# Graph attention on one core: the exponentials of a step issued before that step's node matrices, and the break in the turn of three banks moved from units 15 and 1 to units 11 and 13

## The chip, the cores and the metric

The kernel runs on one core of one Trainium2 chip. A core has a matrix engine (TensorE, in the profile PE, its weight loads PEld), VectorE (DVE), ScalarE (ACT), GpSimd (POOL) and a queue engine (SyncE, SP). Each runs its own list of instructions in order and waits for the others through semaphores. The metric is the time of one execution on the device in microseconds (us). Of the kernel before there are three runs, and one more execution that the profiler watched.

## The reference

The input is a graph of 6250 nodes with 256 features and 106250 edges, sorted by their receiving node. First comes a layer norm, then graph attention with four heads of 64 features, two batch norms with a feed-forward layer between them, and a layer of eight experts. The change lies in the attention:

```python
xl = (x @ W_l).reshape(n, H, C)
xr = (x @ W_r).reshape(n, H, C)
feat = xl[src] + xr[dst]
feat = jnp.where(feat >= 0, feat, NEG_SLOPE * feat)
logits = jnp.einsum('ehc,hc->eh', feat, att)
seg_max = jax.ops.segment_max(logits, dst, num_segments=n)
ex = jnp.exp(logits - seg_max[dst])
seg_sum = jax.ops.segment_sum(ex, dst, num_segments=n)
alpha = ex / (seg_sum[dst] + 1e-16)
out = jax.ops.segment_sum(alpha[:, :, None] * xl[src], dst, num_segments=n)
```

## The kernel before

Edges are packed in tiles of 128, and two tiles that end in the same block of 128 nodes are a unit. Sixteen units are a chunk, and there are 29 chunks. The attention (`attend`) is a software pipeline over steps: step c computes the logits of chunk c, the softmax of chunk c-1, and the weighted sums of chunks c-2 and c-1. Each engine runs its own list of it. A step has sixteen places h = 0 to 15.

- GpSimd gathers the rows `xl[src]` of the two tiles of a unit with two indirect DMAs (L822), five units ahead of the logits. Before that it waits until the sums of the unit that held the same place in the ring are done (`sum_done`).
- SyncE loads the block's rows `xr` (L849).
- ScalarE builds one-hot matrices. For a group of four tiles (a quad, two units) `near_nodes` (L880) and `hot_nodes` (L886) give the node matrix `hot_n`, and `near_edges` (L896) and `hot_edges` (L903) give the edge matrix `hot_e`. `hot_nodes` of quad j waits for `f_done` of the units of quad j-2, since `hot_n` has two buffers. Once a step `exponents` (L921) takes the exponential of the logits less their peak, and `fade_factor` (L925) that by which older sums are scaled down. A step of ScalarE has eight places j, one for two units.
- TensorE at place h makes `logits_of` (L1139 and L1141) for unit h into a PSUM bank of `f_ps`, then `sums_of` (L1154) for an older unit hh = (h + 7) mod 16 into a bank of `o_ps`. At h = 1 it turns the logits (`turn_logits`, L1163) and at h = 6, between logits and sums, the weights (`turn_weights`, L1172 to L1175). The latter waits for the exponentials and the factor.
- VectorE at place h does `settle` (L997, from a bank of `f_ps`), `add_up` (L1034, from a bank of `o_ps`), `messages` (L1021) and `logits_of` (L1007, a reduction). The softmax follows it in three parts at h = 1, 2, 3. The last part ends with L1083, the input of `fade_factor`. At h = 6 VectorE also takes the turned weights (L1014).

`f_ps` and `o_ps` have three banks each. Sixteen is not a multiple of three, so the turn 0, 1, 2 has to break once in a chunk. `slot(h)` says which bank unit h uses, and `freed_by(h)` which earlier unit must have been read by VectorE before TensorE may write that bank. Everywhere but at the break that is the unit three before. With the turn of the kernel before, unit 15 takes bank 1 and waits for unit 13, and unit 1 of the next chunk waits for unit 15: two before in both. Units 0 and 2 wait for the unit four before. The same two functions serve the logits (unit h, at place h) and the sums (unit hh, at place hh - 7 mod 16). `wait_past(pe, settled, ...)` (L1136) and `wait_past(pe, added, ...)` (L1152) are the waits.

Of the kernel before, what the change touches and what calls it, by code (L numbers as in the profile page):

```python
# [37 lines left out]
NU = T // 2  # L38
# [644 lines left out]
def attend(nc, k):  # L683
# [19 lines left out]
    assert NCH % 2 == 1 and NU % LANDS == 0 and T == 32 and NU == 16  # L703


    slot = lambda h: 1 if h == NU - 1 else h % 3
    freed_by = lambda h: h - (4, 2, 4)[h] if h < 3 else h - 2 if h == NU - 1 else h - 3
    with ExitStack() as ctx:
        sb = lambda name, shape, dt=F32: ctx.enter_context(nc.sbuf_tensor(name, shape, dt))
        pb = lambda name, shape: ctx.enter_context(nc.psum_tensor(name, shape, F32))  # L710
# [78 lines left out]
        def has_logits(c):  # L789

            return not isinstance(c, int) or c < NCH

        def softmax_in(c):

            return not isinstance(c, int) or 1 <= c <= NCH

        def behind(c, h, lag):

            b = max(0, -((h - lag) // NU))
            if isinstance(c, int) and not 0 <= c - b < NCH:  # L800
                return None
            return c - b, b, h - lag + b * NU

        def ring_half(engine, c):

            return nc.values_load_multi_w_load_instructions(k.parity[:, bass.ds(c, 2)], engines=[engine], min_val=0, max_val=1)[1]

        with nc.Block(no_gpsimd_drain=True) as block:
# [50 lines left out]
            def _(act):  # L859
# [3 lines left out]
                def relative_rows(c, j):  # L863

                    wait_past(act, far_n_ready, c * QUADS + (j - 2))
                    at = (c * T + j * QT) * P
                    act.dma_start(rel_bc[:, j // 2 % 2].rearrange("p q t e -> p (q t e)"),
                                  k.rel_rows[bass.ds(at, 2 * QT * P)].partition_broadcast(P)).then_inc(rel_in[j // 2 % 2], 16)
# [6 lines left out]
                def near_nodes(c, j):  # L875

                    if j % 2 == 0:
                        act.wait_ge(rel_in[j // 2 % 2], c * (4 * QUADS) + (j // 4 + 1) * 16)
                    wait_past(act, hot_n_ready, c * QUADS + j)
                    nc.scalar.activation(far_n[:, :, :], rel_bc[:, j // 2 % 2, j % 2], ACT.Abs, bias=k.neg_col[:, 0:1]).then_inc(far_n_ready, 1)  # L880

                def hot_nodes(c, j):

                    act.wait_ge(far_n_ready, c * QUADS + (j + 1))
                    wait_past(act, f_done, c * NU + 2 * (j - 1))
                    nc.scalar.activation(hot_n[:, j % 2], far_n[:, :, :], ACT.Relu, scale=-1.0,  # L886
                                         bias=k.one[:, 0:1]).then_inc(hot_n_ready, 1)
# [18 lines left out]
                def linear_parts(c, half):  # L906
                    act.wait_ge(f_done, c * NU)
                    wait_past(act, rows_done, c - 1)
                    act.sem_inc(k.taken, 1)
                    nc.scalar.copy(linear[:, :, :], half.rearrange("p t (h w) -> p h t w", w=XC)[:, :, :, C]).then_inc(linear_ready, 1)  # L910

                def side_masks(c):
                    for i in range(2):
                        nc.scalar.activation(side[:, i], rel_r[:, bass.ds(c - 1, 1), :].rearrange("p o e -> p (o e)"),
                                             ACT.Abs, scale=-1.0, bias=ends[:, i, bass.ds(c - 1, 1)]).then_inc(sides_ready, 1)
                    act.wait_ge(sides_ready, 3 * c - 1)
                    nc.scalar.activation(side[:, :, :], side[:, :, :], ACT.Copy, scale=-NEG).then_inc(sides_ready, 1)

                def exponents(c):
                    act.wait_ge(soft, (c - 1) * SOFT + 12)  # L920
                    nc.scalar.activation(expo[:, 0], below_peak[:, :], ACT.Exp).then_inc(expo_ready, 1)  # L921

                def fade_factor(c):
                    act.wait_ge(soft, (c - 1) * SOFT + 14)
                    nc.scalar.activation(faded[:, :], off_lane[:, :], ACT.Exp, bias=fade[:, 0:1]).then_inc(faded_ready, 1)  # L925

                def step(c):
                    soft_in = softmax_in(c)
                    if isinstance(c, int):
                        other, ring = (c + 1) % 2, xl_e[:, (c + 1) % 2 * T:(c + 1) % 2 * T + T, :]  # L930
                    else:
                        other = ring_half(mybir.EngineType.Activation, c)[1]
                        ring = xl_e.rearrange("p (s t) w -> p s t w", s=2)[:, bass.ds(other, 1)].rearrange("p o t w -> p (o t) w")
                        other = bass.ds(other, 1)
                    for j in range(QUADS):
                        last = j + 1 == QUADS
                        quad = (c + last, (j + 1) % QUADS) if has_logits(c + last) else None
                        edges = behind(c, 2 * j + 3, SUM)
                        if edges:
                            edges = edges[0], edges[2] // 2  # L940
                        if quad:
                            near_nodes(*quad)
                            hot_nodes(*quad)
                            if quad[1] % 2:
                                ahead = (quad[0] + (quad[1] + 3) // QUADS, (quad[1] + 3) % QUADS)
                                if has_logits(ahead[0]):
                                    relative_rows(*ahead)
                        if soft_in and j == 0:
                            linear_parts(c, ring)
                            side_masks(c)  # L950
                        if soft_in and j == 3:
                            exponents(c)
                            fade_factor(c)
                        if edges:
                            near_edges(*edges)
                        if edges:
                            hot_edges(*edges)
                        if has_logits(c) and j == 3:
                            gates_of(c)
                        if j == 4 and has_logits(c + 1):  # L960
                            if not isinstance(c, int) or c > 0:
                                act.wait_ge(f_done, c * NU)
                            target = idx[:, other, :]
                            nc.scalar.copy(target if isinstance(c, int) else target.rearrange("p o t -> p (o t)"),
                                           k.src_e[:, bass.ds((c + 1) * T, T)]).then_inc(idx_ready, 1)
# [4 lines left out]
                near_nodes(0, 0)  # L970
                hot_nodes(0, 0)
                steps_alone(act, step)

            @block.vector
# [1298 lines left out]
```

## Time and profile before

| | |
|---|---|
| three runs | 2504.38, 2498.19, 2502.48 us, median 2502.48 us |
| the profiled execution | 2508.43 us, its span 2506.6 us, granted clock 0.886 |
| busy in the span: PE, DVE, ACT, POOL | 79%, 60%, 48%, 48% |
| indirect gathers L822 | 928, 960 ns each |
| logits' matmuls L1139, L1141 | 1856 and 1856, 391 and 402 ns |
| settle L997, messages L1021, reduction L1007 | 464 each, 681, 679, 681 ns |

Matmuls overlap, so a PE that is busy may still be idle in parts. "idle before" in a row is the time in which that engine did nothing before the instruction, and the name behind it is what ended it by the profile. "issue" and "remote" stand where the profile names no engine.

### The profile page before, as it was taken

The numbers are of one execution on the slowest core, as the hardware profiler recorded it, in microseconds if no ns is written. First come the engines' busy times: TensorE is split into PE (matmuls) and PEld (weight loads), VectorE is DVE, ScalarE is ACT, GpSimd is POOL, SyncE is SP. The second block draws the span as 40 slices with busy tenths as digits, with TensorE's granted clock in tenths as the row PEclk, the third lists the DMA queues.
The fourth block names the chain that finished last, engine by engine and source line by source line (L and its number), as shares of the span: only waits on it lengthen the run. The fifth ranks groups of instructions, "written<-read, shape, count | busy, mean of one in ns | idle before, by whom it ended". The sixth has DMA issues, their size and how long they took to land. (4 is left out here: it accounts for less than half of the span.)

```text
span 2506.6 us, 43475 instructions
## 1 busy us (share of the span) xinstructions
PE 1984.4 (79%) x9692; PEld 1690.5 (67%) x9693; DVE 1516.3 (60%) x3638; ACT 1191.0 (48%) x2805; POOL 1214.0 (48%) x1207
## 2 busy tenths in 40 slices
PE   2974788878888888878888888887886626999996
PEld 2763666767777676767676776667875525888885
DVE  5964777777777777777778777788456440111110
ACT  2542555555555555555555555655545412232321
POOL 3346656555666556655656565520002551344444
PEclk9988998998989899998989899988985557999998
DMA  7675666666666666666666666626602335666664
GB/s 210 228 250 180 193 186 195 185 188 183 194 187 188 180 189 191 194 182 188 189 184 195 176 191 187 190 68 188 204 7 90 108 120 166 136 145 141 144 143 76
DMA packets 256713, 422.34 MB, mean 168 GB/s; under 512 B 45802, under 2 KB 128089, under 8 KB 256653
## 3 DMA queue, kind: packets, MB, share of 16 engines
q1 hardware_dynamic: 154608, 223.36, 28.4%
q0 software_dynamic: 65408, 153.31, 24.9%
q10 hardware_dynamic: 36636, 45.00, 5.6%
q8 instruction: 23, 0.38, 0.1%
q14 instruction: 38, 0.30, 0.0%
HBM read 358.65 MB, written 62.86 MB: 168 GB/s over the span
## 5 line engine op out<-in xcount | busy, mean ns | idle before, releaser
L822 POOL DMA_INDIRECT ring<-xl_rows,a_idx x928 | 890.5, 960 | 594.1 <-issue 272.4
L1139 PE MATMUL a_f_ps<-a_xr_w,a_hot_n 128*128 128x256 f32 x1856 | 571.4, 391 | 177.1 <-DVE a_pos L997 77.8
L1141 PE MATMUL a_f_ps<-ring,ident 128*128 128x256 f32 x1856 | 591.3, 402 | 0.4 <-issue 0.4
L1139 PEld LDWEIGHTS a_f_ps<-a_xr_w,a_hot_n 128*128 128x128 f32 x1856 | 368.0, 203 | 280.5 <-issue 165.1
L1154 PE MATMUL a_o_ps<-ring,a_hot_e 128*128 128x264 f32 x1856 | 535.3, 415 | 19.4 <-issue 13.4
L1154 PEld LDWEIGHTS a_o_ps<-ring,a_hot_e 128*128 128x128 f32 x1856 | 377.0, 207 | 94.0 <-issue 26.5
L997 DVE SCALAR_TENSOR_TENSOR a_pos<-a_f_ps,att_cols 128x512 f32<-128x512 f32 x464 | 316.2, 681 | 190.8 <-remote 120.9
L903 ACT ACTIVATE a_hot_e<-a_far_e,one 128x512 f32<-128x512 f32 x232 | 167.6, 723 | 444.0 <-PE a_o_ps L1154 247.2
L1007 DVE TENSOR_REDUCE a_lg<-a_pos 128x8 f32<-128x512 f32 x464 | 316.0, 681 | 25.2 <-remote 14.9
L1021 DVE TENSOR_TENSOR ring<-ring,a_sm_ps (+1 forms) x464 | 315.2, 679 | 1.7 <-issue 1.7
L1141 PEld LDWEIGHTS a_f_ps<-ring,ident 128*128 128x128 f32 x1856 | 305.6, 202 | 1.2 <-issue 1.1
L896 ACT ACTIVATE a_far_e<-iota_row,a_near_rel 128x128 f32<-128x128 f32 x928 | 294.9, 389 | 4.6 <-issue 3.4
L1034 DVE TENSOR_TENSOR acc<-a_o_ps,acc 128x264 f32 x464 | 198.0, 427 | 159.9 <-PE a_o_ps L1154 80.4
L2033 POOL DMA_INDIRECT out_dram<-ring,x_idx x106 | 166.0, 1566 | 262.8 <-issue 125.1
L886 ACT ACTIVATE a_hot_n<-a_far_n,one 128x512 fp32r<-128x512 f32 x232 | 167.7, 723 | 199.0 <-remote 90.6
L2152 DVE CAST x_idx<-ring 128x2 int32<-128x2 f32 x53 | 9.1, 171 | 386.8 <-PE x_y_ps L2079 386.8
L2079 PE MATMUL x_y_ps<-we,ring 128*128 x848 | 191.6, 379 | 0.0
L2069 PE MATMUL x_hid_ps<-ring,x_w 128*128 128x256 f32 x784 | 177.2, 379 | 0.0
L880 ACT ACTIVATE a_far_n<-a_rel_bc,neg_col 128x512 f32<-128x512 bf16 x232 | 164.9, 711 | 23.1 <-issue 19.5
L2079 PEld LDWEIGHTS x_y_ps<-we,ring 128*128 128x128 f32 x848 | 157.1, 190 | 19.3
L2069 PEld LDWEIGHTS x_hid_ps<-ring,x_w 128*128 128x128 f32 x784 | 149.0, 190 | 20.3
L2111 ACT COPY ring<-x_zt_ps 128x512 f32<-128x512 f32 x53 | 31.1, 586 | 249.7 <-PE x_zt_ps L2047 170.0
(349 smaller groups left out, 2206.3 us busy)
## 6 DMA issues: line engine op xcount, KB each, us to landing
a_xr_w<-xr_rows SPq DMA_DIRECT2D x464, 256.0 KB
a_rel_bc<-rel_rows ACTq DMA_DIRECT2D x116, 256.0 KB
x_w<-in_L_ffn_W_dram SPq DMA_DIRECT2D x57, 512.0 KB, 4.2
ring<-xl_rows,a_idx POOLq DMA_INDIRECT x928
xr_rows<-xr_parts SPq DMA_DIRECT2D x50, 256.0 KB, 2.1
ring<-disp_rows SPq DMA_DIRECT2D x49, 257.0 KB
xl_rows<-xl_sb SPq DMA_DIRECT2D x50, 132.0 KB, 1.8
j_xl<-xl_rows SPq DMA_DIRECT2D x25, 264.0 KB, 2.9
```

The lines of the kernel that those rows point to most:

```text
L822: nc.gpsimd.indirect_dma_start(xl_e[:, p * T + 2 * h + u, :], None, k.xl_rows, bass.IndirectOffsetOnAxis(ap=idx[:, p, 2 * h + u:2 * h + u ...
L886: nc.scalar.activation(hot_n[:, j % 2], far_n[:, :, :], ACT.Relu, scale=-1.0, bias=k.one[:, 0:1]).then_inc(hot_n_ready, 1)
L896: nc.scalar.activation(far_e[:, u, :], k.iota_row[:, :], ACT.Abs, bias=near_rel[:, j * QT + u:j * QT + u + 1]).then_inc(far_e_ready, 1)
L997: nc.vector.scalar_tensor_tensor(pos[:, h % 2], f_ps[:, slot(h)], 0.0, att, ALU.max, ALU.mult).then_inc(settled, 1)
L1007: nc.vector.tensor_reduce(lg[:, :, 2 * h:2 * h + 2].rearrange("p h t -> p t h"), pos[:, h % 2].rearrange("p t (h c) -> p t h c", c=C), AX. ...
L1021: nc.vector.tensor_tensor(at[:, :, :, 0:C], at[:, :, :, 0:C], exs_of(sm)[:, 2 * hh:2 * hh + 2, :, None].to_broadcast([P, 2, H, C]), ALU.mu ...
L1034: nc.vector.tensor_tensor(at, o_ps[:, slot(hh), 0:XW], at, ALU.add).then_inc(added, 1)
L1139: nc.tensor.matmul(f_ps[:, slot(h), u, :], hot_n[:, j % 2, 2 * g + u, :], xr_w[:, h % XR, a, :].bitcast(F32R), start=(a == 0), stop=False)
L1141: last = nc.tensor.matmul(in_heads(f_ps[:, slot(h), u, :]), k.ident[:, :], heads_of(xl_e[:, p * T + 2 * h + u, :])[:, :, 0:C], start=False ...
L1154: last = nc.tensor.matmul(o_ps[:, slot(hh), 0:XW], hot_e[:, j % 2, 2 * g + u, :], xl_e[:, pp * T + 2 * hh + u, :], start=(u == 0), stop=(u ...
L2069: last = nc.tensor.matmul(hid_ps[:, q % 2, j], w1[:, q % RING, h, j * P:(j + 1) * P], zt[:, q % 2, h], start=(h == 0), stop=(h == DH - 1))
L2079: last = nc.tensor.matmul(y_ps[:, q % 2, u], hid[:, q % 2, j, u * P:(u + 1) * P], k.we2[:, bass.ds(e[u], 1), j, :].rearrange("p o n -> p ( ...
```

## The change

Two edits, both in the attention.

The first moves the calls of `exponents(c)` and `fade_factor(c)` in ScalarE's place j = 3. They stood behind `near_nodes` and `hot_nodes` of quad 4, and now stand ahead of them. The second gives `slot` and `freed_by` a start of the turn behind unit 11. Unit 12 has bank 0, 13 bank 1, and so on over the chunk's end, up to unit 10 with bank 2; unit 11 has bank 1. So unit 11 now waits for unit 9 and unit 13 for unit 11 (two before), units 12 and 14 for the unit four before, and all others, 15 and 1 too, for the unit three before. It holds for logits and sums alike.

```diff
-    slot = lambda h: 1 if h == NU - 1 else h % 3
-    freed_by = lambda h: h - (4, 2, 4)[h] if h < 3 else h - 2 if h == NU - 1 else h - 3
+    CLOSE = 11
+    turn_of_slots = lambda h: (h - CLOSE - 1) % NU
+    slot = lambda h: 1 if h == CLOSE else turn_of_slots(h) % 3
+    freed_by = lambda h: h - (4, 2, 4)[turn_of_slots(h)] if turn_of_slots(h) < 3 else h - 2 if h == CLOSE else h - 3
...
                         quad = (c + last, (j + 1) % QUADS) if has_logits(c + last) else None
+                        if soft_in and j == 3:
+                            exponents(c)
+                            fade_factor(c)
                         edges = behind(c, 2 * j + 3, SUM)
...
                             side_masks(c)
-                        if soft_in and j == 3:
-                            exponents(c)
-                            fade_factor(c)
                         if edges:
                             near_edges(*edges)
```

On ScalarE, in the repeated step, this is what stands between the edge matrix of place j = 2 and the edge matrices of place j = 3 in the kernel before:

```order
L903 ACTIVATE a_hot_e<-a_far_e,one 128x512 [waits a_sum_s]
L878 REGISTER_ALU
L880 ACTIVATE a_far_n<-a_rel_bc,neg_col 128x512 [waits a_hot_n_s,a_rel_in0]
L884 REGISTER_ALU
L125 REGISTER_ALU [waits a_far_n_s]
L886 ACTIVATE a_hot_n<-a_far_n,one 128x512 [waits a_f_s]
L920 ISA
L921 ACTIVATE a_expo<-a_below_peak 128x128 [waits a_soft]
L924 REGISTER_ALU
L925 ACTIVATE a_faded<-a_off_lane,a_fade 128x5 [waits a_soft]
L125 REGISTER_ALU
```

And in the changed kernel (its lines are two further down):

```order
L905 ACTIVATE a_hot_e<-a_far_e,one 128x512 [waits a_sum_s]
L922 ISA
L923 ACTIVATE a_expo<-a_below_peak 128x128 [waits a_soft]
L926 REGISTER_ALU
L927 ACTIVATE a_faded<-a_off_lane,a_fade 128x5 [waits a_soft]
L880 REGISTER_ALU
L882 ACTIVATE a_far_n<-a_rel_bc,neg_col 128x512 [waits a_hot_n_s,a_rel_in0]
L886 REGISTER_ALU
L125 REGISTER_ALU [waits a_far_n_s]
L888 ACTIVATE a_hot_n<-a_far_n,one 128x512 [waits a_f_s]
L125 REGISTER_ALU
```

The two exponentials, which wait for VectorE's softmax (`a_soft`), have moved past the node matrix, which waits for TensorE's logits (`a_f_s`). No DMA moved past another.

On TensorE, at place h = 6 of the repeated step, the kernel before has this between the logits of unit 6 and those of unit 7:

```order
L1139 MATMUL a_f_ps<-a_xr_w,a_hot_n 128x256 x2
L1141 MATMUL a_f_ps<-ring,ident 128x256
L1171 ISA [waits a_expo_s,a_faded_s,a_soft,a_masks]
L1172 MATMUL a_sm_ps<-a_faded,a_spot 128x5 [waits a_spot_s]
L1173 MATMUL a_sm_ps<-a_lane,a_spot 128x5
L1175 MATMUL a_sm_ps<-ident,a_expo 128x128 x2
L1154 MATMUL a_o_ps<-ring,a_hot_e 128x264 [waits a_added,a_msg_s]
L1154 MATMUL a_o_ps<-ring,a_hot_e 128x264
```

The changed kernel has there:

```order
L1141 MATMUL a_f_ps<-a_xr_w,a_hot_n 128x256 x2
L1143 MATMUL a_f_ps<-ring,ident 128x256
L1170 REGISTER_ALU [waits a_masks]
L1173 ISA [waits a_faded_s,a_expo_s,a_soft]
L1174 MATMUL a_sm_ps<-a_faded,a_spot 128x5 [waits a_spot_s]
L1175 MATMUL a_sm_ps<-a_lane,a_spot 128x5
L1177 MATMUL a_sm_ps<-ident,a_expo 128x128 x2
L1156 MATMUL a_o_ps<-ring,a_hot_e 128x264 [waits a_added,a_msg_s]
L1156 MATMUL a_o_ps<-ring,a_hot_e 128x264
```

No matmul moved. What the second edit changes is the bank that a matmul writes and the count that it waits for, which these rows don't tell.

## Rows read from the trace of the kernel before

**Rows 1.** Busy time in windows: steps 2 to 27, then step 24 alone.
```profile
core 0: us, PE busy (x) PEld busy (x) DVE busy (x) ACT busy (x) POOL busy (x), PEclk, DMA share, GB/s
282.10:1613.00 1330.90, 1090.90 (x5254) 921.04 (x5253) 1019.50 (x2158) 736.65 (x1664) 796.26 (x831) 0.91 0.64 188
1413.10:1460.00 46.90, 39.88 (x205) 33.63 (x203) 37.52 (x82) 27.88 (x64) 28.81 (x31) 0.96 0.67 201
```
**Rows 2.** Who waited for whom over the whole span: us in total, times, longest.
```profile
POOL ring L822 <- PE a_o_ps L1154: 227.6, 115, 2.8
PEld a_sm_ps L1172 <- issue: 120.4, 29, 5.7
ACT a_hot_n L886 <- remote: 90.6, 18, 10.1
PE a_f_ps L1139 <- DVE a_pos L997: 77.8, 27, 10.0
```
**Rows 3.** Timeline of step 20, places 5 to 7: start, us, instruction, idle before.
```profile
1225.67 0.15 DVE L1083 TENSOR_TENSOR a_fade<-a_reach_t,a_peak 128x1 f32<-128x1 f32 x1
...
1228.44 0.72 ACT L886 ACTIVATE a_hot_n<-a_far_n,one 128x512 fp32r<-128x512 f32 x1 [7.33 <-remote]
...
1229.27 0.28 ACT L925 ACTIVATE a_faded<-a_off_lane,a_fade 128x5 f32<-128x5 f32 x1
...
1229.78 0.59 PE L1172 MATMUL a_sm_ps<-a_faded,a_spot 128*128 128x5 f32 x2 [5.07 <-ACT a_faded L925]
...
1232.51 1.00 PE L1139 MATMUL a_f_ps<-a_xr_w,a_hot_n 128*128 128x256 f32 x2
...
1233.40 0.43 DVE L1034 TENSOR_TENSOR acc<-a_o_ps,acc 128x264 f32 x1 [2.14 <-PE a_o_ps L1154]
```
**Rows 4.** Timeline of step 3, the same place.
```profile
355.25 0.15 DVE L1083 TENSOR_TENSOR a_fade<-a_reach_t,a_peak 128x1 f32<-128x1 f32 x1
...
355.98 0.38 PE L1172 MATMUL a_sm_ps<-a_faded,a_spot 128*128 128x5 f32 x2 [1.70 <-DVE a_expo L1082]
...
357.39 0.70 PE L1139 MATMUL a_f_ps<-a_xr_w,a_hot_n 128*128 128x256 f32 x2
```
**Rows 5.** The same pair in the first and last of the steps 2 to 27.
```profile
302.91 0.15 DVE L1083 TENSOR_TENSOR a_fade<-a_reach_t,a_peak 128x1 f32<-128x1 f32 x1
...
306.91 0.59 PE L1172 MATMUL a_sm_ps<-a_faded,a_spot 128*128 128x5 f32 x2 [4.96 <-ACT a_faded L925]
...
1584.28 0.15 DVE L1083 TENSOR_TENSOR a_fade<-a_reach_t,a_peak 128x1 f32<-128x1 f32 x1
...
1587.69 0.58 PE L1172 MATMUL a_sm_ps<-a_faded,a_spot 128*128 128x5 f32 x2 [4.36 <-ACT a_faded L925]
```
**Rows 6.** Timeline of step 20: settle 13 and logits 15, then step 21, logits 1.
```profile
1251.99 0.68 DVE L997 SCALAR_TENSOR_TENSOR a_pos<-a_f_ps,att_cols 128x512 f32<-128x512 f32 x1
...
1252.73 0.51 PE L1139 MATMUL a_f_ps<-a_xr_w,a_hot_n 128*128 128x256 f32 x2 [0.92 <-issue]
...
1260.46 0.68 DVE L997 SCALAR_TENSOR_TENSOR a_pos<-a_f_ps,att_cols 128x512 f32<-128x512 f32 x1
...
1261.29 0.47 PE L1139 MATMUL a_f_ps<-a_xr_w,a_hot_n 128*128 128x256 f32 x2 [2.24 <-issue]
...
1261.99 0.69 DVE L1007 TENSOR_REDUCE a_lg<-a_pos 128x8 f32<-128x512 f32 x1
...
1263.12 0.64 PE L1163 MATMUL a_sm_ps<-ident,a_lg 128*128 128x128 f32 x2
```
**Rows 7.** Step 20: logits 13 and settle 11 (places 13 and 11).
```profile
1247.01 0.59 PE L1139 MATMUL a_f_ps<-a_xr_w,a_hot_n 128*128 128x256 f32 x2
...
1247.74 0.68 DVE L997 SCALAR_TENSOR_TENSOR a_pos<-a_f_ps,att_cols 128x512 f32<-128x512 f32 x1
```
**Rows 8.** Step 20: sums 11 and add 9 (places 4 and 2).
```profile
1218.31 1.05 PE L1154 MATMUL a_o_ps<-ring,a_hot_e 128*128 128x264 f32 x4
...
1219.80 0.42 DVE L1034 TENSOR_TENSOR acc<-a_o_ps,acc 128x264 f32 x1
```

## The prediction, made before the changed kernel ran

> **What bounds the kernel now.** I read the busy times in windows first. The attention's steps 2 to 27 take 1330.9 us together, which is 51.2 us for each of 26 steps and half of the span; nothing outside the attention is changed. TensorE is busy 1090.9 us of them, VectorE 1019.5, GpSimd 796.3, ScalarE 736.7 [rows 1]. None is busy all the time: the engines take turns waiting for each other. One step of the 26 took only 46.9 us with the same work [rows 1], so the waits can be smaller without any work being removed. The list of waits says where they are [rows 2]. TensorE's sequencer stood 120.4 us before the turn of the weights (L1172), once in each of 29 steps, 4.15 us each time. TensorE stood 77.8 us more before the logits' matmuls for VectorE's settle, and ScalarE 90.6 us before `hot_nodes`, on a signal that the profile gives no engine for. The reader is to see that the turn of the weights is the largest single stop of TensorE, and that it depends on an instruction that ScalarE has queued behind `hot_nodes`.
>
> The timeline of step 20 shows why [rows 3]. VectorE ends the softmax's last part at 1225.82 (1225.67 + 0.15). ScalarE is free, but its next instruction is `hot_nodes`, which starts at 1228.44 after 7.33 us of standing; only then come the exponential and the factor (ends 1229.55), and the turn starts at 1229.78, 3.96 us after the softmax's end. VectorE then loses 2.14 us before its `add_up` at place 6, whose matmuls are queued behind the turn. In step 3 the same way from the softmax's end (355.40) to the turn (355.98) took 0.58 us [rows 4]. That is the shortest that I find, and what an exponential without another wait ahead of it costs.
>
> **Edit 1, the exponentials first.** Over the 26 steps the way from softmax's end to the turn is 2.03 us in the mean: 3.85 in the first, 3.26 in the last [rows 5], 0.57 to 0.60 in 8 of them and more in 18. With `exponents` ahead of `near_nodes` and `hot_nodes` the only thing ahead that waits for TensorE is the edge matrix of place 2, and with that step 20's ScalarE was done by 1221.11 (1228.44 - 7.33). So the way falls to about 0.58 everywhere: 2.03 - 0.58 = 1.45 us a step, 42 us for 29 steps. Bounds: nothing, if what VectorE and TensorE do next starts no earlier; and 120.4 us, all of the stop before the turn, which it can't reach because most of the stop is the softmax itself. What the edit delays is the node matrix of quad 4. It takes two instructions of about 0.72 us, so it would end some 1.8 us after the softmax's end. Its first reader is the logits of unit 8, and before these come the turn, sums 13, logits 7 and sums 14; in step 20 the turn alone to logits 7 is 1229.78 to 1232.51, 2.7 us [rows 3]. That covers it, and I cost it at nothing. If the cover were gone, each step would lose at most the 1.4 us of the two instructions.
>
> How much of the 1.45 us arrives at the end? TensorE stands ahead of the turn, so it starts sums 13 earlier by all of it. VectorE waits there for sums 13 in the steps of the late kind (2.14 us in step 20, rows 3) and not in the others. Against this I set the lengths of whole steps: the 8 steps with the short way took 49.8 us in the mean, the 18 others 52.2. The difference of 2.4 us is even a little more than the 2.1 us by which their ways differ (2.68 - 0.58), though other things differ in these steps too. So I take the full 42 us.
>
> **Edit 2, the break of the turn.** Four places of TensorE wait for a bank at the break: logits 15 and 1 and sums 15 and 1 before, logits 11 and 13 and sums 11 and 13 now.
> - Logits 15 (waits for settle 13). In step 20 settle 13 ends at 1252.67 and logits 15 starts at 1252.73 after 0.92 us of idling [rows 6]. In all 26 steps it starts 0.05 us after that settle, and the idling is 1.92 us in the mean. This wait goes; the next is settle 12.
> - Logits 1 (waits for settle 15). In step 21 settle 15 ends at 1261.14, logits 1 starts at 1261.29 after 2.24 us. So it is in 18 of 26 steps, mean idle 1.70 us. This wait goes too, but the turn of the logits (L1163) is behind it in the queue and needs the reduction of unit 15, which ends at 1262.68; the turn starts at 1263.12 [rows 6]. At most 0.44 us is to be had here in that step, 0.24 in most.
> - Logits 13 (now waits for settle 11). In step 20 it starts at 1247.01 and settle 11 ends at 1248.42 [rows 7]. In all 26 steps logits 13 started before that settle's end, by 1.41 us in the mean. So TensorE will stand about 1.4 us there, more if edit 1 makes it earlier. From logits 13 to the point where TensorE is ready for logits 15 it is 4.80 us (1252.73 - 0.92 - 1247.01) in step 20, and settle 13 ends 4.25 us after settle 11. So in such a step logits 15 would start about 0.5 us later than now, not earlier. Where VectorE has stood between settle 11 and settle 13 (9 of 26 steps have an idle of 2.8 us or more ahead of logits 15) TensorE no longer stands with it, and I put that at 2 us. The mean is (9 x 2 - 17 x 0.5) / 26 = 0.37 us gained, rounded to 0.3.
> - Logits 11 (now settle 9) has 0.99 us to spare in the mean and would wait in 6 of 26 steps. Sums 13 (now add 11) has 1.98 us to spare.
> - Sums 11 (now waits for add 9). In step 20 it starts at 1218.31 and add 9 ends at 1220.22 [rows 8]; it started early in 23 of 26 steps, by 1.30 us in the mean. The delay passes to logits 5, sums 12 and logits 6. All of that is in front of the turn of the weights, where TensorE stands 4.15 us now and would still stand 4.15 - 1.45 = 2.7 us with edit 1. So it is hidden.
>
> Bounds for the whole edit: the two waits that go are worth at most 1.92 + 0.24 = 2.2 us a step; the two that come cost at most 1.41 + 1.30 = 2.7. I take the 0.3 us a step from logits 15, 9 us, close to nothing, because the wait at 13 gives back most of what the wait at 15 took.
>
> **The sum.** 42 + 9 = 51 us off the profiled execution's 2508.4 (its span is 2506.6, so 1.8 us lie around it): 2457. The median of the three runs is 6 us lower, so the same saving gives 2502.5 - 51 = 2451. Since both terms lean to their favourable side I name 2455.
>
> **Rivals.**
> - *The clock comes back* (larger gain). After 5.07 us of standing the first matmul pair of logits 7 takes 1.00 us where a pair takes 0.5 elsewhere [rows 3, 6], and from the turn to logits 7 it is 2.73 us against 1.41 us in step 3, where TensorE stood 1.70 us [rows 3, 4]. Those are the levels of 1.2 and 2.4 GHz; the granted clock is 0.91 over the steps and 0.96 in the quickest one [rows 1]. With the stop split between sums 11 and a shorter wait at the turn, 1.3 us more a step come back, 38 us: 2413. Against it: VectorE has to use the earlier sums. The Trainium skill, TensorE: Matmul & The Clock Gate, "What's actually happening", says "the default state is throttled, and activity releases the throttle". By that rule shorter stops give clock back, which is this rival; the rows just named agree.
> - *Hidden anyway* (no change). GpSimd stood 227.6 us for sums that TensorE had to signal [rows 2], and in step 20 ScalarE got the signal of logits 5 only at 1228.4, although TensorE had been through with logits 6 since 1224.71 (1229.78 - 5.07, rows 3). If these late signals set the pace of everything, the turn comes earlier and VectorE waits for the next signal instead: 2500. For it: 7.33 us of waiting in rows 3 are not explained by work. Against: the short-way steps are shorter.
> - *The wait at 13 and 11 costs* (slower). Place: logits 13 and sums 11. TensorE's lead over VectorE is cut to two units there, and if late signals reach VectorE meanwhile it runs dry. Price: 1.41 + 1.30 - 0.3 - 0.24 = 2.2 us a step, 63 us. It decides when edit 1 brings less than that, because sums 11 isn't hidden: with the 42 us in full the sum is +21 us, 2523. It needs sums 11 to delay settle 4 or the softmax; in step 20 VectorE reached the softmax's end without waiting for TensorE, which speaks against it.
> - *The exponential is late for another reason* (the edit doesn't do what it says): the edge matrix ahead of it waits for TensorE as well, and if its signal is as late as that of `hot_nodes`, half of the 42 us are lost: 2475. This lies within the forecast's own range.
>
> **How the numbers follow.** Forecast (with the last rival) 0.46, own range 2430 to 2485; clock 0.15, 2395 to 2430; hidden 0.19, 2485 to 2510; slower 0.20, 2510 to 2545. The likeliest gives 2455. From 2412 to 2520 leaves out about 1 in 10 on each side. No change can be told from one within 0.3%, that is 2495 to 2510. Faster: 0.46 + 0.15 + 0.06 of the hidden case = 0.67; same 0.12; slower 0.21.
>
> **What would show it.** Right: the way from L1083's end to the turn is near 0.6 us in all steps; the sequencer's stop before the turn falls from 120 to about 75 us; logits 15 and 1 start without idling and logits 13 starts 0.05 us after settle 11; the steps average 49.4 us. Wrong in edit 1: the turn is early but VectorE's idle time per step is unchanged, or ScalarE's exponential waits behind the edge matrix. Wrong in edit 2: sums 11's wait lengthens the way to the softmax, or VectorE idles more at places 13 to 15 than before.

## The result and the profile after

The changed kernel takes 2484.74 us (median of 4 runs, 2481.26 to 2486.9) beside 2503.43 us for the kernel before (4 runs, 2498.19 to 2504.71): a ratio of 0.9932, 95% interval 0.9912 to 0.9952. It is faster by 18.7 us, 0.7%. The forecast was 2455 us, 48 us less than before. The profiled execution took 2486.9 us, its span is 2485.1 us, the granted clock 0.904.

The same kernel before took 2479 to 2503 us in some groups of runs (called late below; the result above and the profile ahead of the prediction are of this kind) and 2156 to 2158 us in others (called quick), whatever version ran beside it, so every ratio below is within one group.

Busy time in the changed kernel's windows, the 26 steps and then step 20, in the columns of [rows 1]:

```profile
280.69:1596.63 1315.94, 1057.66 (x5254) 891.77 (x5253) 1016.62 (x2161) 740.55 (x1665) 796.45 (x833) 0.95 0.64 190
1194.71:1243.96 49.25, 39.01 (x205) 33.62 (x203) 37.57 (x82) 27.67 (x63) 29.42 (x32) 0.97 0.64 188
```

A step is 50.61 us in place of 51.19: the 26 steps give 15.0 of the 21.5 us between the spans, the steps and drains around them 4.4, the rest of the program 2.2. The granted clock rose from 0.91 to 0.95 and TensorE is busy 33 us less, but VectorE's idle time fell only from 11.98 to 11.51 us a step.

The list of waits of the changed kernel answers to [rows 2]:

```profile
POOL ring L824 <- PE a_o_ps L1156: 195.7, 112, 2.9
...
PE a_f_ps L1141 <- DVE a_pos L999: 97.4, 38, 10.7
...
PEld a_sm_ps L1174 <- issue: 49.5, 24, 4.8
```

TensorE's sequencer stands 49.5 us before the turn of the weights where it stood 120.4. TensorE's wait for the settle rose from 77.8 to 97.4. The waits moved from the turn to the logits.

The timeline of step 20 around the softmax answers to [rows 3]:

```profile
1215.21 0.31 ACT L923 ACTIVATE a_expo<-a_below_peak 128x128 f32<-128x128 f32 x1 [2.07 <-issue]
1215.30 0.15 DVE L1085 TENSOR_TENSOR a_fade<-a_reach_t,a_peak 128x1 f32<-128x1 f32 x1
...
1216.02 0.38 PE L1174 MATMUL a_sm_ps<-a_faded,a_spot 128*128 128x5 f32 x2 [1.31 <-ACT a_expo L923]
```

In this step ScalarE waits for the softmax and not for TensorE. The turn starts 0.57 us after the softmax's end (1215.45), where it took 3.96 us before, and the node matrix follows at once (1216.50). The edit does what it says. But seven microseconds later in the same step:

```profile
1222.98 0.59 PE L1143 MATMUL a_f_ps<-ring,ident 128*128 128x256 f32 x2
...
1225.20 0.59 PE L1143 MATMUL a_f_ps<-ring,ident 128*128 128x256 f32 x2
...
1228.04 0.96 POOL L824 DMA_INDIRECT ring<-xl_rows,a_idx  x1 [0.30 <-issue]
1230.84 0.69 DVE L999 SCALAR_TENSOR_TENSOR a_pos<-a_f_ps,att_cols 128x512 f32<-128x512 f32 x1 [3.24 <-remote]
1230.84 0.72 ACT L888 ACTIVATE a_hot_n<-a_far_n,one 128x512 fp32r<-128x512 f32 x1 [3.62 <-remote]
1231.58 0.80 PE L1141 MATMUL a_f_ps<-a_xr_w,a_hot_n 128*128 128x256 f32 x2 [4.89 <-DVE a_pos L999]
1231.75 0.95 POOL L824 DMA_INDIRECT ring<-xl_rows,a_idx  x1 [2.75 <-remote]
```

TensorE ended logits 9 at 1223.57 and logits 10 at 1225.79. VectorE's settle of unit 9 waits for that signal until 1230.84, 7.3 us after the work, and ScalarE's node matrix is let go at the same moment. Logits 11, which after edit 2 waits for settle 9, stands 4.89 us behind it. The trace has the two signals at 1230.81 and 1230.96. They came while GpSimd had stopped (1229.00 to 1231.75), after an unbroken row of eight gathers.

Counted over the 416 units of steps 2 to 27, by the records of TensorE's signals for logits (some records of late ones are missing): 115 of 416 are on time, that is within 0.3 us of the matmul's modelled end. Of those due in the first 1.3 us of a row of gathers 29 of 42 are, of those due 3.9 us or more into a row none of 168. Of 215 late arrivals on record 196 fall in a stop of GpSimd, 1.7 us (median) after its last gather ended. All 50 settles ahead of which VectorE idled over 1.5 us started in such a stop or less than 1 us behind it; they are 5.7 us a step. In the kernel before it was 122 of 416 on time and 38 such settles, 4.6 us a step.

The Trainium skill, Perfetto Trace Analysis, "Tensor Engine Instruction (MATMUL, LD_WEIGHTS)", says that the matmul's end in a trace is an estimate and that the signal goes out later. That alone doesn't explain 7.3 us here: TensorE's next logits followed 2.2 us after logits 9, at the usual pace, and where signals are on time they are within 0.3 us of that estimated end.

### The profile page after: what moved, and what is told of

Read it like the earlier page. It is cut to its first block and busy times, and to the rows that moved or that the text cites. A ratio compares the mean times of both kernels' runs of the same rounds, so it can differ in the third digit from the quotient of the medians.

```text
span 2485.1 us, 43501 instructions
## 1 busy us (share of the span) xinstructions
PE 1949.5 (78%) x9692; PEld 1661.9 (67%) x9693; DVE 1512.5 (61%) x3638; ACT 1193.7 (48%) x2805; POOL 1211.4 (49%) x1207
## 2 busy tenths in 40 slices
DMA packets 256712, 422.34 MB, mean 170 GB/s; under 512 B 45801, under 2 KB 128088, under 8 KB 256652
## 5 line engine op out<-in xcount | busy, mean ns | idle before, releaser
L1141 PE MATMUL a_f_ps<-a_xr_w,a_hot_n 128*128 128x256 f32 x1856 | 572.5, 391 | 156.4 <-DVE a_pos L999 97.4
L1156 PE MATMUL a_o_ps<-ring,a_hot_e 128*128 128x264 f32 x1856 | 521.9, 406 | 60.1 <-DVE acc L1036 35.9
L1156 PEld LDWEIGHTS a_o_ps<-ring,a_hot_e 128*128 128x128 f32 x1856 | 364.1, 201 | 140.1 <-issue 79.7
```

The costliest lines, as they stand in the source:

```text
L1141: nc.tensor.matmul(f_ps[:, slot(h), u, :], hot_n[:, j % 2, 2 * g + u, :], xr_w[:, h % XR, a, :].bitcast(F32R), start=(a == 0), stop=False)
L1156: last = nc.tensor.matmul(o_ps[:, slot(hh), 0:XW], hot_e[:, j % 2, 2 * g + u, :], xl_e[:, pp * T + 2 * hh + u, :], start=(u == 0), stop=(u ...
```

## GpSimd's row of gathers and its stops

The gathers' own group, in the kernel before and then in the changed one. Behind the bar stand busy us and mean ns of one, behind the next bar the idle time ahead of them and what ended it.

```profile
L822 POOL DMA_INDIRECT ring<-xl_rows,a_idx x928 | 890.5, 960 | 594.1 <-issue 272.4 <-PE a_o_ps L1154 227.6 <-remote 80.4
```
```profile
L824 POOL DMA_INDIRECT ring<-xl_rows,a_idx x928 | 888.1, 957 | 578.8 <-issue 248.5 <-PE a_o_ps L1156 195.7 <-remote 121.8
```

Busy and idle together fell from 1484.6 to 1466.9 us, 17.7 of the 21.5 us between the spans. A gather shows 0.96 us and then 0.30 of "issue" even within a row, so 32 gathers take GpSimd 40.4 us a step (1.262 us each). In the 26 steps it counts as busy for 60% (796.3 of 1330.9 us), but the gathers with these gaps are 79% of a step. With its stops (idle over 0.6 us, each counted beyond the 0.30) this gives the step:

| kernel, late groups | stops a step | their time | 40.4 + stops | step measured |
|---|---|---|---|---|
| before | 6.6 | 10.70 | 51.1 | 51.19 |
| changed | 5.7 | 10.21 | 50.6 | 50.61 |
| changed, second group | 5.4 | 10.04 | 50.4 | 50.49 |
| exponentials alone | 5.3 | 10.12 | 50.5 | 50.43 |
| break alone | 5.8 | 9.81 | 50.2 | 50.17 |
| lead limited | 5.5 | 10.48 | 50.9 | 50.76 |

This is bookkeeping and not a cause: the gathers and the idle time between them fill a step whatever sets its length, so the sum would come out in any version. The experiments without gathers test the cause.

## The experiments

### The edits taken apart, quick group

All cuts of code are against the changed kernel unless said otherwise. The exponentials alone (edit 1, the turn of banks as before):

```diff
-    CLOSE = 11
-    turn_of_slots = lambda h: (h - CLOSE - 1) % NU
-    slot = lambda h: 1 if h == CLOSE else turn_of_slots(h) % 3
-    freed_by = lambda h: h - (4, 2, 4)[turn_of_slots(h)] if turn_of_slots(h) < 3 else h - 2 if h == CLOSE else h - 3
+    slot = lambda h: 1 if h == NU - 1 else h % 3
+    freed_by = lambda h: h - (4, 2, 4)[h] if h < 3 else h - 2 if h == NU - 1 else h - 3
```

> Edit 1 alone: the exponentials ahead of the node matrices, the break of the turn at units 15 and 1 as before. Theory A (the late signals set the pace): TensorE's wait before the turn of the weights shrinks by about 2.6 us a step as in the changed kernel, but VectorE's idle time stays near 12 us a step, and the time falls by 5 to 15 us only, ratio 0.994 to 0.998. Theory B (edit 1 brings its full 42 us and edit 2 costs half of it back): ratio near 0.983. Theory C (the gain of the changed kernel is edit 2's): ratio 1.000.

The break alone (edit 2, the exponentials behind `hot_nodes` as before):

```diff
-                        if soft_in and j == 3:
-                            exponents(c)
-                            fade_factor(c)
                         edges = behind(c, 2 * j + 3, SUM)
...
+                        if soft_in and j == 3:
+                            exponents(c)
+                            fade_factor(c)
                         if edges:
                             near_edges(*edges)
```

> Edit 2 alone: the break at units 11 and 13, the exponentials behind the node matrices as before. Theory A: a few us either way, ratio 0.996 to 1.002. Theory B: slower by 20 to 25 us, ratio 1.008 to 1.010. Theory C: faster by 19 us, ratio 0.993.

Both edits, but only the logits' break moved, then only the sums' (`slot` and `freed_by` take one of the two starts each):

```diff
-    CLOSE = 11
+    CLOSE_F, CLOSE_O = 11, 15
...
```

> Both edits, but the sums' banks keep the old break (sum units 15 and 1); only the logits' banks break at 11 and 13. TensorE's wait before sums 11 (1.62 us a step in the changed kernel) is gone, the waits before logits 11 and 13 stay. If the wait before sums 11 is hidden before the turn of the weights, as I predicted, the ratio is that of the changed kernel, 0.993; if it costs its 1.6 us a step, 47 us less: ratio 0.975.

```diff
-    CLOSE = 11
+    CLOSE_F, CLOSE_O = 15, 11
...
```

> Both edits, but the logits' banks keep the old break (15 and 1); only the sums' banks break at 11 and 13. TensorE waits before logits 15 and 1 again and no longer before logits 11 and 13. If the logits' break costs the same wherever it stands, the ratio is 0.993; if moving it gave the 19 us, 1.000; if moving it cost the missing half of edit 1, 0.985.

Measured, beside 2156.05 us for before: 2156.33 (ratio 1.0001, 0.9992 to 1.001), 2154.04 (0.9991, 0.9982 to 1.0), 2156.19 (0.9999, 0.9989 to 1.0008) and 2154.22 us (0.9991, 0.9982 to 1.0). In that order these are the exponentials alone, the break alone, the logits' break and the sums' break. No part is worth more than some 0.2% by these intervals. The windows of the exponentials alone, in the same columns, and its gathers:

```profile
260.49:1310.61 1050.12, 998.89 (x5254) 836.28 (x5253) 1010.84 (x2160) 739.34 (x1666) 796.68 (x833) 1.00 0.81 238
...
L822 POOL DMA_INDIRECT ring<-xl_rows,a_idx x928 | 889.7, 959 | 289.9 <-issue 252.2 <-PE a_o_ps L1154 28.6 <-ACT a_idx L861 7.5
```

A step is 40.39 us, GpSimd's 32 gathers at 1.26 us with no stop over 1 us in 26 steps: one unbroken row. All 416 signals are on time all the same. TensorE never stands before the turn (0.00 us, and 0.00 too in the break alone, which has the exponentials in their old place), and before logits 15 and 1 it stands 0.01 and 0.07 us, so there is no wait for either edit to remove. The forecast was about the late kind, and this group can't test its 42 us. The changed kernel as it is, with both breaks moved, was not run in a quick group. Between the late trace of the kernel before and this quick one GpSimd's idle time ahead of its gathers falls from 594.1 to 289.9 us, 304 of the 350 us between the spans, for the same gathers.

### The same apart, late groups

The changed kernel once more and the exponentials alone in one late group:

> The changed kernel itself against the kernel before, on the chip of these experiments. In the first comparison the kernel before took 2503 us and its engines' register instructions often took 0.7 us (321 of them between 0.6 and 0.8 us); in the first four experiments the same kernel took 2156 us with none of them, and each half of the change gave a ratio of 1.000. Theory D: where the signals are quick, GpSimd's gathers pace the step (32 x 1.26 us = 40.4 us), and the change gives nothing: ratio 0.999 to 1.001 if the kernel before takes about 2156 us. Where it takes about 2500 us the ratio is 0.993. Rival: both halves are needed together, and the changed kernel is faster on either: ratio 0.993.

> Edit 1 alone again. If the kernel before takes about 2500 us here, theory A (the late signals set the pace) expects 0.994 to 0.998 and theory B (edit 2 costs half of edit 1's gain) 0.983. If it takes about 2156 us, both expect 1.000 again, and the repetition says how well these numbers hold.

Beside 2497.57 us the changed kernel took 2479.43 (0.9924, 0.9909 to 0.9939), the exponentials alone 2483.03 (0.9941, 0.9924 to 0.9958). So edit 1 by itself is worth 14.5 us (10 to 19 by the interval) and not 42, as theory A of the first expectation had it. The trace shows two places where the rest went. The first is ahead of the turn itself, here in step 20:

```profile
1210.48 0.15 DVE L1083 TENSOR_TENSOR a_fade<-a_reach_t,a_peak 128x1 f32<-128x1 f32 x1
1210.51 0.72 ACT L903 ACTIVATE a_hot_e<-a_far_e,one 128x512 f32<-128x512 f32 x1 [5.23 <-remote]
1211.14 0.29 ACT L921 ACTIVATE a_expo<-a_below_peak 128x128 f32<-128x128 f32 x1
...
1211.86 0.38 PE L1172 MATMUL a_sm_ps<-a_faded,a_spot 128*128 128x5 f32 x2 [1.98 <-ACT a_faded L925]
```

The exponential now stands behind the edge matrix of place 2, and that one waited 5.23 us for a late signal of the sums. In 18 of 26 steps it is so: the exponential starts after the softmax's end, behind an edge matrix that had waited 4.7 to 5.9 us. The way from softmax to turn is 0.98 us in the mean, not 0.58. With both edits no exponential starts late in this manner, and the way is 0.65 us. The second place is logits 1, which still waits for settle 15 here:

```profile
1243.61 0.68 DVE L997 SCALAR_TENSOR_TENSOR a_pos<-a_f_ps,att_cols 128x512 f32<-128x512 f32 x1
...
1244.44 0.77 PE L1139 MATMUL a_f_ps<-a_xr_w,a_hot_n 128*128 128x256 f32 x2 [3.38 <-DVE a_pos L997]
```

GpSimd stood from 1240.09 to 1242.58 there. Over 26 steps TensorE's stop before the turn fell from 3.98 us a step (the kernel before, whose trace is of another late group) to 1.71, and the one before logits 1 rose from 1.70 to 3.26. That is 1.56 of 2.27 us handed on.

The break alone was run in four groups, three of them quick (the first is above):

> The second edit alone (break at units 11 and 13, exponentials where they were). Where the kernel before takes about 2500 us: the exponentials alone gave 0.9941 there and both edits 0.9924, so if the two add, the break alone gives about 0.998, some 4 us faster. If the new waits at logits 13 and 11 and sums 11 cost what they show as TensorE's idle time (1.4, 2.3 and 1.6 us a step, against 1.9 and 1.7 us that go), it is 1.6 us a step or 46 us slower, 1.018. If late signals set the pace whatever the waits are, 1.000. Where the kernel before takes about 2156 us: 1.000 again.

> The second edit alone, hoped for on a chip where the kernel before takes about 2500 us. If the two edits add (exponentials alone 0.9941, both 0.9924), the break alone gives about 0.998. If the new waits at logits 13 and 11 and sums 11 cost what they show as TensorE's idle time, it is about 1.018. If late signals set the pace whatever the waits are, 1.000. Where the kernel before takes about 2156 us: 1.000.

> The second edit alone, hoped for on a chip where the kernel before takes about 2500 us. If the two edits add, about 0.998; if the new waits at logits 13 and 11 and sums 11 cost what they show as idle time, about 1.018; if late signals set the pace whatever the waits are, 1.000. Where before takes 2156 us: 0.999 to 1.000.

In the quick ones it took 2158.32 (0.9995, 0.9986 to 1.0004) and 2154.48 us (0.9989, 0.998 to 0.9998). In the late one 2468.61 us beside 2479.23: 0.9952, 0.9934 to 0.9971, 10.6 us faster. None of the three expectations names that: it is more than adding up gives, and the new waits don't cost what they show as idle time. The trace has them, though: logits 11 idles 2.03 us, logits 13 0.80, sums 11 1.20 a step, logits 15 and 1 0.03 and 0.10. TensorE's stop before the turn is smaller too, 2.40 us beside 3.98, with the exponentials in their old place (again two groups, 2479 and 2503 us). This suggests that the two edits remove partly the same standing time: 14.5 and 10.6 us alone, 18 to 19 together and not 25. It is not shown, since the intervals of the two parts (10 to 19 and 7 to 16 us) leave room for a sum of 19, and they are too wide to order the three versions.

The sums' break alone with the exponentials ahead, again a quick group:

> Both edits, but only the sums' break at units 11 and 13; the logits' stays at 15 and 1. On a chip where the kernel before takes about 2500 us: if the logits' move brought the gain of the second edit (the wait at 15 goes), this one falls back to the exponentials alone, 0.994. If the waits at logits 11 and 13 cost and the sums' move brings the gain, it beats the changed kernel, 0.990. If all is set by late signals, it is 0.992 to 0.994. On a quick one 1.000.

It took 2157.48 us, 0.9998 (0.9988 to 1.0007). Which of the two breaks gives edit 2's gain was not measured in a late group and stays open.

### A shorter lead for the gathers

```diff
                         pool.wait_ge(sum_done, c * NU + (h - RING + 1))
+                    PACE = 4
+                    wait_past(pool, f_done, c * NU + (h - PACE + 1))
```

> The changed kernel, with GpSimd's gather of unit n also waiting for the logits of unit n - 4, so that it can't run seven units ahead. If long rows of gathers are what delays the signals, shorter rows mean shorter delays: faster by 1 to 3 per cent where the kernel before takes 2500 us. Rival: the gathers are then late for TensorE, and it is slower by 1 per cent or more. Where the kernel before takes 2156 us theory D expects 1.000 to 1.01, since GpSimd paces the step and any wait more is added.

In the late group with 2497.57 us it took 2484.31 us (0.9939, 0.9919 to 0.9959), 5 us over the changed kernel there, which the two intervals don't tell apart. It did not break the rows up: there are still 5.9 gathers in a row and 140 of 416 signals on time. It was expected faster by 1 to 3 per cent or slower by 1 or more, and neither came. The added wait hangs on the same late signals.

### The gathers taken off GpSimd

The changed kernel in which SyncE loads each tile of `xl` as 128 consecutive rows with an ordinary DMA, so that other rows of the table are read. The bytes (422.85 MB beside 422.34) and the readers are the same, in more and smaller packets (345,862 beside 256,712), and GpSimd issues nothing in the attention:

```diff
-                for h in range(LEAD):
-                    gather(0, 0, h)
-                steps(pool, step)
+                pool.sem_inc(k.taken, 1)
...
+                            near = k.xl_rows.rearrange("(b p) w -> b p w", p=P)[bass.ds(row_of[g], 1)].rearrange("o p w -> (o p) w")
+                            for u in range(2):
+                                sp.dma_start(xl_e[:, p * T + 2 * h + u, :], near).then_inc(landed[h % LANDS], 16)
```

> The changed kernel without its gathers on GpSimd: SyncE loads, for each tile, 128 consecutive rows of the same table (the block of the unit) by an ordinary DMA. The rows are not the edges' rows, so it isn't the same computation, but bytes moved and everything else are as before. Theory D: the step falls below 40.4 us to what VectorE's work allows, about 39 us, where the kernel before takes 2156 us; where it takes 2500 us the 0.7 us register instructions and the late signals vanish with GpSimd's gathers, and the time falls to about 2100 us. Rival E (the late signals have nothing to do with the gathers): where the kernel before takes 2500 us they remain, and the time stays above 2400 us.

In the late group it took 2130.21 us beside 2497.57 (0.8526, 0.8511 to 0.8541). The step is 38.74 us and all 416 signals are on time. With the gathers gone the late signals are gone. But this also changes which rows are read and removes GpSimd's pace, so in the next kernel GpSimd keeps half:

```diff
-                        if has_logits(c + more):
+                        if has_logits(c + more) and (h + LEAD) % 2 == 0:
                             gather(c + more, (p + more) % 2, (h + LEAD) % NU)
...
+                            if h % 2:
...
+                                for u in range(2):
+                                    sp.dma_start(xl_e[:, p * T + 2 * h + u, :], near).then_inc(landed[h % LANDS], 16)
```

> The changed kernel, in which only the even units are gathered by GpSimd; the tiles of the odd units come by SyncE's ordinary DMAs as 128 consecutive rows of the same table (so other rows are read for them). If TensorE's signals are held back by rows of GpSimd's gathers, half the gathers leave gaps in which they come through: on a chip where before takes 2500 us the step falls below 44 us and the time below 2300, toward the 2130 us that no gather at all gave. If it is the amount of data or the engines' own waits, the data are the same and the time stays at 2480. On a quick chip, where 32 gathers of 1.26 us set the step of 40.4 us, it falls to some 2110 us.

> The changed kernel, in which only the even units are gathered by GpSimd; the tiles of the odd units come by SyncE's ordinary DMAs as 128 consecutive rows (so other rows are read for them). On a chip where before takes 2500 us: if rows of GpSimd's gathers hold TensorE's signals back, below 2300 us; if it is the amount of data or the engines' own waits, 2480 us. Where before takes 2156 us: 2097 us, as measured there.

> The changed kernel with half the gathers (the even units on GpSimd, the odd ones as 128 consecutive rows by SyncE), hoped for on a chip where the kernel before takes about 2500 us. If rows of GpSimd's gathers hold TensorE's signals back, below 2300 us; if it is the amount of data or the engines' own waits, 2480 us. Where before takes 2156 us: 2097 us once more.

Quick: 2096.81 us beside 2158.2 (0.9717, 0.9703 to 0.9732) and 2097.22 us beside 2156.48 (0.9726, 0.9711 to 0.974). Late: 2127.34 us beside 2479.23, 0.858 (0.8565 to 0.8595). Half the gathers take away not half of the loss in the attention but all of it: the step is 38.75 us in both kinds of group. The 30 us left between 2127 and 2097 us lie behind the attention (803.1 us from its last sum to the end beside 770.7 in `half_2`), and so do the 38 us between the late and quick runs of the changed kernel without any gathers (806 beside 769). The windows (steps 2 to 27, one step) and the gathers in the late group:

```profile
241.73:1249.36 1007.63, 973.75 (x5255) 847.22 (x5253) 999.49 (x2160) 740.00 (x1666) 398.66 (x416) 1.00 0.82 248
939.36:978.12 38.76, 37.46 (x205) 32.56 (x203) 38.44 (x85) 28.43 (x65) 15.32 (x16) 1.00 0.82 249
```
```profile
940.54 0.96 POOL L824 DMA_INDIRECT ring<-xl_rows,a_idx  x1 [2.23 <-PE a_o_ps L1162]
941.80 0.96 POOL L824 DMA_INDIRECT ring<-xl_rows,a_idx  x1 [0.30 <-issue]
945.42 0.96 POOL L824 DMA_INDIRECT ring<-xl_rows,a_idx  x1 [2.66 <-PE a_o_ps L1162]
```

GpSimd still issues 16 gathers a step, but in rows of about two, and at least 340 of 416 signals are on time. VectorE is busy 38.44 of 38.76 us: it is the bound that is left. The DMA engines move 248 GB/s, more than in [rows 1] (188), so it isn't the amount of data. In late groups the lateness hangs on the gathers. That it is the length of a row and not the number of gathers rests only on the counts within one trace (29 of 42 on time early in a row, none of 168 late in one), for this kernel changes both.

One rival is not separated: a gather is an instruction on GpSimd and a transfer on its own queue, and both experiments take away both. In the changed kernel the queue's last packet ends 1.5 us (median) after the last gather's instruction of a row, close to the 1.7 us at which the signals come. So the transfers may hold the signals back as well as the instructions.

### The edits without gathers

The kernel before with no gathers on GpSimd (the same edit as above), in two quick groups, and the changed one beside it:

> The kernel before, with none of the gathers on GpSimd: the tiles of all units come by SyncE's ordinary DMAs as 128 consecutive rows of the same table. The changed kernel without the gathers took 2130 us. If the exponentials' place matters by itself (a way from softmax to turn of 1.9 us in place of 0.6 us, with no late signals), this takes up to 1.3 us a step more, 2167 us. If the change only ever worked on what the gathers held back, it is the same, 2130 us.

> The kernel before with no gathers on GpSimd (128 consecutive rows for each tile by SyncE). On a chip where before takes 2500 us the changed kernel without gathers took 2130 us. If the exponentials' place matters by itself, this takes up to 1.3 us a step more, 2167 us; if the change only worked on what the gathers held back, the same as the next run, within 0.3%.

> The changed kernel with no gathers on GpSimd, on the same chip as the kernel before without them. Both theories: about 2130 us on a chip where before takes 2500 us, and about 2095 us where it takes 2156. Against the run before it, it tells what the change is worth when nothing is gathered: 0 to 38 us.

The first took 2094.56 us (0.9707, 0.9692 to 0.9722). In the other group before without gathers took 2093.81 us (0.9715, 0.97 to 0.9731) and the changed kernel without them 2092.26 (0.9708, 0.9694 to 0.9723): no difference. The way from softmax to turn is 0.58 us in both, wherever the exponentials stand, because `hot_nodes` hardly waits (1.2 us in all over the 26 steps of the kernel before without gathers). All this was seen only in quick groups: what the edits would be worth without gathers in a late one was not measured.

## Why the prediction was wrong

- **"The way falls to about 0.58 everywhere."** Right for the changed kernel: 0.65 us in the mean, over 1 us in one step of 26. The sequencer's stop fell further than said (120 to 49.5, not to 75), and the cover of the node matrix held. With edit 1 alone it was not: 0.98 us. The rival *the exponential is late for another reason* came true there, the edge matrix ahead of the exponential waiting for a late signal. It cost 0.40 of the 1.45 us a step, 12 of the 42 us.
- **"So I take the full 42 us."** This is the step that failed. Measured were 14.5 us for edit 1. That the turn came earlier did not bring the next steps earlier by as much, because TensorE then stood for another late signal: 1.56 of the 2.27 us gained before the turn came back before logits 1. I took the full amount from the steps with a short way being shorter, 49.8 against 52.2 us. The second number is wrong: the 18 others took 51.8 us (8 x 49.8 + 18 x 51.8 is the 1331 us of [rows 1]), so the difference is 2.0 us and not 2.4, a little less than the 2.1 us of the ways. Even so it prices nothing. With a way of 0.65 in all steps they still run from 47.75 to 54.07 us (46.93 to 56.22 before). In the kernel before the length of a step goes with the time of the stops of GpSimd that begin in it (correlation 0.84) more than with the way (0.48). But a longer step holds more stop time in any case, and in the two traces of the changed kernel the same correlation is 0.83 and 0.39, so this is a hint at most.
- **"Hidden anyway"** named the mechanism that the runs bear out, with a chance of 0.19, and gave it too much: part of the gain did arrive. I counted against it the same short steps. The 227.6 us of GpSimd's waiting for sums [rows 2] was in my hands and is part of the same standing time.
- **The range.** 2484.74 us lie inside my 2430 to 2485, at its very edge. That is luck and speaks for nothing: the saving was 18.7 us where 48 were named, and "hidden" began at 2485.
- **The clock** came back partly (0.91 to 0.95; from the turn to logits 7 1.75 us in place of 2.54). TensorE was busy 33 us less in 26 steps, but they became only 15 us shorter, since TensorE's idle time rose from 9.23 to 9.93 us a step.
- **Edit 2, the waits.** Logits 15 and 1 start without idling (0.00 and 0.10 us), as said. Sums 11 idles 1.66 us (1.30 said) and logits 13 1.42 (1.41). Logits 11 was to wait in 6 of 26 steps, waits in 21 and idles 2.26 us in the mean: late signals reached it. 9 us were forecast, and alone it measured 10.6. That agreement is luck, for the 9 us were to come at logits 15 alone, and TensorE's stops moved in six places. Beside edit 1 it adds some 4 us (2483.03 to 2479.43), within the intervals.
- **The slower rival** fell: the waits at 13 and 11 are there at the named size, and the break alone was faster by 10.6 us all the same.
- **The sum.** 42 + 9 = 51 us was off in its first term by 27 us. That the two terms don't add, because they draw on the same standing time, fits the times but is within their intervals.

What is shown: in late groups TensorE's signals are late with all the gathers on GpSimd and on time with half of them or none, and where signals are on time no part of the change gains more than some 0.2%. A row of gathers alone is not enough for it, since in quick groups the row is unbroken and all signals are on time. What is only argued is that the gain left over comes through fewer and shorter stops of GpSimd: no run set the stops by themselves. Why one and the same program meets late signals in one group and not in another stays open. So does what the attention would take with all its gathers in short rows. Since 32 of them need 40.4 us a step and half of them left 38.75, it could not reach the 2127 us of half the gathers: 29 x 1.65 = 48 us more give 2175 us at best, an estimate.

## What to carry to other kernels

Before a wait is priced, ask whether its signal left when its work ended: where the waiting engine stood idle, its start less the end of the instruction it waits for tells (7.3 us here), and where that is large, a wait that is removed can come back at the next reader of a late signal. For an engine that issues DMAs take the pace from start to start (1.26 us) and not from busy time (0.96): 60% busy was 79% of the step. Steps that differ together don't price an edit; a step's length has to be compared with every stop in it, not only with the one in question.

## What the hardware showed that was not expected

- In late groups TensorE's signals for logits reached the other engines almost only in the first microseconds of a row of indirect gathers or in its pause: 0 of 168 on time beyond 3.9 us into a row, 4 of 143 in the kernel before. With two gathers in a row at least 340 of 416 came on time. In quick groups all 416 came on time within one unbroken row.
- In the same groups the trace has some 320 (before) and 370 (changed) register instructions of 0.6 to 0.8 us on ScalarE, VectorE and SyncE; in quick ones it has none. In late groups without gathers it has 9, all behind the attention, and with half the gathers 58, though signals are on time there, so such instructions alone don't make signals late.
- The same kernel took 2156.48 us in one group and 2479.23 us in another under the same chip number, so it doesn't look like a property of the chip alone.
- One indirect gather of 128 rows keeps GpSimd for 1.26 us from start to start at best (0.96 us of it shown as busy), in late and quick groups alike.
